# One value product moved in front of the first scores of each attention segment

## The reference

```
q = (x @ w_q).reshape(B, Sq, HEADS, DIM_HEAD).transpose(0, 2, 1, 3)
k = (context @ w_k).reshape(B, Skv, HEADS, DIM_HEAD).transpose(0, 2, 1, 3)
v = (context @ w_v).reshape(B, Skv, HEADS, DIM_HEAD).transpose(0, 2, 1, 3)
sim = jnp.einsum('bhid,bhjd->bhij', q, k) * SCALE
attn = jax.nn.softmax(sim, axis=-1)
out = jnp.einsum('bhij,bhjd->bhid', attn, v)
return out.transpose(0, 2, 1, 3).reshape(B, Sq, INNER) @ w_o + b_o
...
x = x + _L0_xattn_ref(_layernorm(x, axis=-1), ctx_768, ...)
x = x + _L0_ffn_ref(_layernorm(x, axis=-1), ...)
x = x + _L1_xattn_ref(_layernorm(x, axis=-1), ctx_768, ...)
x = x + _L1_ffn_ref(_layernorm(x, axis=-1), ...)
```

## Time and profile before

| | us |
|---|---|
| median of 3 runs | 2785.21 |
| lowest and highest | 2784.88, 2785.31 |
| the profiled execution's own time | 2785.64 |
| its span in the trace | 2784.0 |

### The profile page before, as it was taken

One profiled execution on the slowest core, in us unless ns is written; L12 is line 12 of the kernel. 1 busy time (PEld: TensorE's weight loads), 2 busy tenths in 40 slices (PEclk: granted clock), 3 DMA queues, 4 the chain that ended last, 5 costly groups with the idle time before them and its releaser, 6 DMA issues. The chain is left out here.

```text
span 2784.0 us, 37259 instructions
## 1 busy us (share of the span) xinstructions
PE 2561.1 (92%) x13254; PEld 1783.1 (64%) x13254; DVE 2085.5 (75%) x2464; ACT 1287.2 (46%) x1776; POOL 1495.0 (54%) x1132
## 2 busy tenths in 40 slices
PE   4999999999999689999999689999999999996895
PEld 3656565656565378888888555656565656554784
DVE  5777777787878577777777667777777777765795
ACT  3545554555554333333333354545454545443384
POOL 2867776777686511111111157677777777671345
PEclk9999999999999899999999789999999999997998
DMA  3211211221211100000000021112122121104212
GB/s 108 55 52 43 65 48 52 57 55 42 67 42 48 48 30 28 23 23 23 23 26 19 15 82 49 49 53 56 50 55 59 42 55 43 48 22 157 88 49 89
DMA packets 60160, 141.65 MB, mean 51 GB/s; under 512 B 8448, under 2 KB 21632, under 8 KB 59008
## 3 DMA queue, kind: packets, MB, share of 16 engines
q1 hardware_dynamic: 55184, 132.73, 16.7%
q0 software_dynamic: 1536, 4.20, 0.5%
q10 hardware_dynamic: 3312, 3.02, 0.3%
HBM read 79.36 MB, written 10.22 MB: 32 GB/s over the span
## 5 line engine op out<-in xcount | busy, mean ns | idle before, releaser
L382 POOL TENSOR_TENSOR L0a_psums<-L0a_psums,L0a_probs 128x512 f32<-128x512 f32 x384 | 479.9, 1284 | 20.5 <-ACT L0a_probs L439 20.5
L382 POOL TENSOR_TENSOR L1a_psums<-L1a_psums,L1a_probs 128x512 f32<-128x512 f32 x384 | 479.9, 1284 | 20.3 <-ACT L1a_probs L439 20.3
L520 DVE TENSOR_REDUCE L0a_row_max<-psum 128x2 f32<-128x2048 f32 x128 | 293.6, 2294 | 90.6 <-PE psum L657 89.7
L520 DVE TENSOR_REDUCE L1a_row_max<-psum 128x2 f32<-128x2048 f32 x128 | 293.6, 2293 | 90.4 <-PE psum L657 89.5
L884 POOL TENSOR_TENSOR L0e_w_lo<-L0e_raw,L0e_w_hi 128x768 fp32r<-128x768 f32 x34 | 63.7, 1873 | 497.3 <-ACT L0e_w_hi L898 497.3
L439 ACT ACTIVATE L1a_probs<-psum 128x1024 f32<-128x1024 f32 x256 | 259.7, 1027 | 91.9 <-PE psum L681 91.8
L439 ACT ACTIVATE L0a_probs<-psum 128x1024 f32<-128x1024 f32 x256 | 259.6, 1027 | 91.8 <-PE psum L681 91.8
L938 DVE SCALAR_TENSOR_TENSOR xres<-psum,L0e_weights_of,xres 128x256 f32<-128x256 f32 x544 | 225.6, 477 | 22.5 <-PE psum L1111 21.9
L695 PE MATMUL psum<-L0a_probs,L0a_v 128*64 128x512 f32 x1024 | 242.2, 605 | 0.0
L695 PE MATMUL psum<-L1a_probs,L1a_v 128*64 128x512 f32 x1024 | 240.5, 602 | 0.0
L1097 PE MATMUL psum<-xnT_hi,L0e_w_hi 128*128 128x512 f32 x544 | 214.4, 394 | 5.1 <-DVE L0e_hid L946 4.9
(11 more groups left out here) (357 smaller groups left out, 6151.7 us busy)
## 6 DMA issues: line engine op xcount, KB each, us to landing
L0a_k_hs<-L0a_k_st SPq DMA_DIRECT2D x64, 256.0 KB, 3.6
L1a_k_hs<-L1a_k_st SPq DMA_DIRECT2D x64, 256.0 KB, 3.6
L0a_raw<-in_attention SPq DMA_DIRECT2D x35, 384.0 KB, 3.0
L1a_raw<-in_attention SPq DMA_DIRECT2D x35, 384.0 KB, 3.0
L0e_raw<-in_experts SPq DMA_DIRECT2D x34, 384.0 KB, 3.0
L1weights<-in_sorted SPq DMA_DIRECT2D x2, 6144.0 KB, 18.6
L0a_q_hh<-L0a_q_hh SPq DMA_DIRECT2D x64, 128.0 KB, 2.3
L1a_q_hh<-L1a_q_hh SPq DMA_DIRECT2D x64, 128.0 KB, 2.3
```

The costliest lines, as they stand in the source:

```text
L382: nc.gpsimd.tensor_tensor(psums[:, h, :], a, probs[:, h, kv, :], ALU.add).then_inc(sem["acc"], 1)
L520: nc.vector.reduce_max(row_max[:, qt, 0:2 * 32].rearrange("p (h n) -> p h n", h=2)[:, :, 0], psum[:, 0:4 * BANK].rearrange("p (h k) -> p h ...
```

## The change

`pv(i, 0)` is issued once before the loop over the rounds, and the table loses its 0.

```
--- before.py
+++ after.py
@@ -744,7 +744,8 @@
                             qk(i, 7)
                             if i > 0:
                                 output(i - 1, 1)
-                            FILL = ((0, 1, 2), (), (3, 4, 5), (6, 7))
+                            pv(i, 0)
+                            FILL = ((1, 2), (), (3, 4, 5), (6, 7))
                             for qt in range(QT):
                                 if i + 1 < SEGMENTS:
                                     score(i + 1, qt)
```

## The result

| | before | after |
|---|---|---|
| median, us (6 runs each) | 2785.34 | 2797.10 |
| lowest to highest, us | 2784.88 to 2786.01 | 2795.70 to 2797.48 |
| span of the profiled execution, us | 2784.0 | 2794.0 |

The changed kernel is slower: the ratio of the times is 1.004, with a 95% interval of 1.003 to 1.0051, which is 8 to 14 us. The profiled execution of after took 2795.7 us, at the low end of its runs. All times in this document are of undisturbed executions: one of the nine of a later kernel, fill_empty_round, took 4223.78 us at a granted clock of 0.56 and is left out of its median.

What follows compares the result with a forecast made beforehand. PE was taken to bound the kernel, busy for 92% of the span. Sixty ordinary segments at +0.18 us (10.8) less 0.5 for two first segments gave +10.3 on 2785.2: 2795.5 us, range 2786 to 2800.

Steps and rivals of the forecast that it cites:

- O to product: From the start of the output projection's second half (O) to the moved value product: 0.81 us.
- Product to S0: From the moved product to the next segment's first scores (S0): 0.86 us of passes and a 0.15 turn, 1.01.
- S0 to S1: From first to second scores (S1): 3.12 us, bounded by DVE's reduction, against 3.39 before; upper bound 3.22.
- O to S1: From the output projection's second half to second scores: 4.94 us against 4.76, each ordinary segment 0.18 longer.
- The turn and its weight load: PE's turn from value products to scores, load not done beforehand: 0.15 us, taken ahead of first scores too.
- the rival of 2786.5 us: The weight load ahead of the first scores is hidden: +0.03 us a segment, +1.3 us in total; chance 0.11.
- the one of 2780.5: Between projection and first scores both turns vanish: -0.07 us a segment, the kernel is faster; chance 0.05.
- The third rival: DVE's release of the second scores costs more: round 3.22 us, +0.28 us a segment, 2801.7 us; chance 0.08.
- I price no change of clock: Granted clock is 1.00 in these stretches and PE's idle pieces stay under 0.7 us, so no clock cost.
- 0.2146 for one: Length in us of one value pass, from segment 31's paired weight loads, 0.429 for two; four passes 0.86.
- Whether it was given back later: After the second scores every link starts from them or what follows, so 0.18 us a segment is not recovered.

Runs made afterwards that it cites:

- fill_empty_round: The changed kernel with value products 3 and 4 in segment 30's empty second round and 5 alone in the third: 2792.7 us, beside 2785.01 for the kernel before.
- three_left_in_first_round: The changed kernel with products 1, 2 and 3 in the first round and 4 and 5 in the third: 2811.10 us, beside 2785.01 for the kernel before.
- short_max_after: The changed kernel with DVE's reduction cut to the first head's two banks: 2752.68 us, beside 2791.14 for the kernel before.
- two_in_front: The changed kernel with two products ahead of the first scores and one left in the first round: 2850.52 us, beside 2785.01 for the kernel before.
- the first experiment: The changed kernel with only one head's half of the first product ahead of the first scores, the other half behind: 2809.65 us, beside 2785.01 before.
- short_max_before: The kernel before with DVE's reduction cut to the first head's two banks: 2781.46 us, beside 2791.14 for the kernel before.

## Why the prediction was right

**The sign and the size.** Foreseen was 2795.5 us against 2785.2, +10.3; measured was +11.8. In the trace, which the sum was made for, the span was foreseen at 2794.3 and is 2794.0.

**The three distances.** O to product: 0.81 foreseen, 0.80 found. Product to S0: 1.01 and 1.01. S0 to S1: 3.12 and 3.12. The deciding step, that the first round was PE's by 0.27 us only and would become DVE's, was read off one empty round in segment 30 and was borne out by three_left_in_first_round, short_max_after and two_in_front. O to S1 is longer by 0.17, where 0.18 was foreseen.

**The turn and its weight load.** S0 could have started 0.44 us earlier, and its weight load was still not pulled ahead. With that the rival of 2786.5 us fell, and so did the one of 2780.5. The third rival fell because DVE's release after value products costs 0.06 us.

It is not so that this engine never loads weights ahead over rows in use. In the kernel before, just ahead of O:

```profile
523.18 0.40 PE L681 MATMUL psum<-L0a_q_lm,L0a_k_hs 65*128 65x512 f32 x1
523.19 0.19 PEld L680 LDWEIGHTS psum<-L0a_q_hh,L0a_k_st 128*128 128x128 f32 x1
523.42 0.40 PE L680 MATMUL psum<-L0a_q_hh,L0a_k_st 128*128 128x512 f32 x1
```

The load for 128 rows starts 0.23 us before its own matmul, while a matmul on 65 of these rows has just begun. In the attention of both traces, before and after, the loads are exposed, within 0.03 us of the first matmul, wherever PE changes between scores (64 rows, 128 columns), value products (128 rows, 64 columns) and the full 128 by 128; among matmuls of one of these forms, most loads start ahead. So what goes along with the 0.15 us, and with the 0.10 from the projection to the products, is the change of form; no run varied the form alone. The Trainium skill, page "TensorE: Matmul & The Clock Gate", Part 3, "The mechanism", says in its list of what overlaps that a weight load runs beside a matmul in flight only when their row groups differ. At S0 the trace agrees; in the rows above it doesn't, and the measurement decides. The same section, like Part 2 before it, also names loads to a background weight buffer as pulled ahead; no run here tells where a load goes.

**What I had not foreseen.** After S1 the keys round is 0.02 us shorter (3.17 to 3.15). Before, it was 3.19 in every second segment and 3.15 in the others; now it is 3.15 to 3.16 in all. Why was not settled. It gives back some 1 us in all.

**What was wrong.** "I price no change of clock": I looked at ordinary segments only the earlier trace rows and not at segment 30, whose empty round I used for another number. That PE's idle pieces stay under 0.7 us was wrong by my own rows: segment 30 has 2.39 and segment 0 has 1.20. In segment 30 the clock already fell in one layer of the kernel before, and it falls in both after: 1.7 us of the span's 10.0. My two misses, 0.03 us a segment too much (1.8 us) and this left out, went against each other: that the forecast span is within 0.3 us of the measured one is luck. Further, "0.2146 for one" pass was the wrong reading of a right row: four passes of two heads take 0.86 us, but as two pairs side by side. The sum used whole products only and was not touched; the first experiment built on a half one was.

**Whether it was given back later.** It was not: transposes to the next O stayed at 12.92 and third scores to transposes at 6.87.

## What to carry to other kernels

Before filling a hole on the bounding engine, set the whole filler, with the turns to and from it, against the hole: here 1.11 us (0.10 for the turn, 0.86 and 0.15) went into 0.66. Then ask how much shorter the place that it leaves can get before another engine bounds it: here 0.27 us of 0.86. If both answers are less than the piece, cut the piece, and cut it along a dimension that costs time: columns streamed, not heads that run side by side.

## What the runs showed of the hardware

- Value products of plain float32 (128 x 64) whose results go to different halves of the partitions run beside each other: one head's two passes of 512 columns took 1.00 us up to the next scores, both heads' four took 1.01, and four passes of 256 columns 0.58.
- The granted clock can fall on short idle times: after 2.39 us of idle time in segment 30 it was 0.58 to 0.64 over the next 4.4 to 5.0 us in nine of fourteen layers, and 1.00 in the other five. In short_max_before the same slow passes followed an idle piece of 1.21 us in segment 0, and no fall followed one of 1.32 us in segment 30. What else decides it was not found.
- From the end of DVE's reduction to PE's next scores it was 0.05 to 0.06 us where the round was DVE's, and from the end of ACT's exponential 0.15 us.
- Weight loads of full 128 by 128 products mostly started 0.12 to 0.23 us ahead of their matmuls, also over rows in use; where the form of the matmuls changed they started with the first matmul. Such turns cost 0.15 us from value products to scores and 0.10 from the output projection to value products.
